# Attention stage: the scaled addition of the fetched expert results moves from VectorE to GpSimd, and the statistics after it one step later

## The reference, cut to what matters

```python
x = x + L0_attn(layernorm(x))
x = x + (y + shared)         # y: sum over a token's two experts of weight * expert result
x = x + L1_attn(layernorm(x))
x = x + L1_ffn(layernorm(x))
```

## Time and profile before

| what | value |
|---|---|
| median of 3 runs | 1394.51 us (1394.25 to 1395.08) |
| profiled execution | 1400.14 us |
| its span, first to last instruction | 1398.1 us |
| mean granted TensorE clock | 0.988 of full speed |
| busy: PE / DVE / ACT / POOL | 1336.1 / 688.0 / 489.1 / 448.3 us |

### The profile page before, as it was taken

How to read it: one execution, slowest core, us unless ns; L and a number is a source line. 1 busy time by engine, 2 the same in 40 slices (tenths; PEclk the granted TensorE clock), 3 DMA queues, 4 the chain that set the end, 5 groups by cost and what they waited for, 6 DMA issues and landing times.

```text
span 1398.1 us, 25005 instructions
## 1 busy us (share of the span) xinstructions
PE 1336.1 (96%) x8348; PEld 1036.2 (74%) x8348; DVE 688.0 (49%) x2499; ACT 489.1 (35%) x1046; POOL 448.3 (32%) x541
## 2 busy tenths in 40 slices
PE   7899999999999999999999999999998999999998
PEld 5566556688998998656666666666666788999998
DVE  5655457233333333337878888888887231310000
ACT  2221211122222222113666666666755412111111
POOL 2100000253222221242454454544323524343332
PEclk9999999999999999998999999999999999999999
DMA  9402011067777777243554554645442779999996
GB/s 327 129 31 72 4 41 43 22 220 234 234 243 238 237 236 226 67 120 100 143 155 140 148 154 130 181 116 150 146 128 75 273 289 312 346 333 344 332 347 210
DMA packets 95676, 254.29 MB, mean 182 GB/s; under 512 B 12189, under 2 KB 42271, under 8 KB 85568
## 3 DMA queue, kind: packets, MB, share of 16 engines
q1 hardware_dynamic: 79728, 217.61, 47.8%
q0 software_dynamic: 12096, 32.13, 7.4%
q10 hardware_dynamic: 3728, 2.97, 0.7%
HBM read 201.42 MB, written 52.17 MB: 181 GB/s over the span
## 4 chain that ended last, share of the span: by engine, by line
PE 84%; DVE 8%; issue 4%; ACT 2%; DMA 0%; DVEq 0%; ACTq 0%; POOLq 0%
PE psum L994 10%; PE psum L1004 10%; PE psum L675 10%; PE psum L813 10%; PE psum L796 7%; PE psum L686 6%; PE psum L851 4%; PE psum L898 4%; PE psum L873 4%; PE psum L922 3%; DVE work L1892 3%; PE psum L823 2%; PE psum L956 2%; PE psum L768 2%; PE psum L933 2%
## 5 line engine op out<-in xcount | busy, mean ns | idle before, releaser
L1892 DVE CUSTOM_DVE_ANT_0 work<-psum,mask 128x384 bf16<-128x384 f32 (+1 forms) x512 | 230.6, 485 | 59.3 <-PE psum L851 57.6
L851 PE MATMUL psum<-kz,qT 96*128 96x384 f32 (+1 forms) x512 | 167.3, 398 | 10.6 <-DVE small L1892 9.5
L1971 POOL DMA_INDIRECT work<-normed,token_of x71 | 67.5, 951 | 325.1 <-PE psum L768 198.2
L813 PEld LDWEIGHTS psum<-work,arena 128*128 128x128 f32 x1136 | 136.1, 193 | 15.7 <-ACT work L1148 11.0
L675 PE MATMUL psum<-arena 128*128 128x512 f32 x320 | 147.7, 600 | 0.0
L813 PE MATMUL psum<-work,arena 128*128 128x128 f32 x1136 | 143.6, 280 | 4.0 <-ACT work L1148 2.2
L994 PEld LDWEIGHTS psum<-arena 128*128 128x128 f32 x1248 | 145.5, 192 | 2.4 <-issue 0.4
L994 PE MATMUL psum<-arena 128*128 128x128 f32 x1248 | 146.2, 275 | 0.0
L1244 ACT ACTIVATE arena<-psum 128x384 f32<-128x384 f32 x256 | 112.2, 494 | 93.7 <-PE psum L873 92.8
L1004 PE MATMUL psum<-arena 128*128 128x256 f32 x624 | 143.1, 383 | 0.5 <-issue 0.5
L1746 DVE TENSOR_TENSOR arena<-psum,arena 128x256 f32<-128x256 f32 x39 | 16.6, 425 | 245.8 <-PE psum L1004 245.8
(11 more groups left out here) (243 smaller groups left out, 1993.0 us busy)
## 6 DMA issues: line engine op xcount, KB each, us to landing
arena<-in_w SPq DMA_DIRECT2D x78, 1024.0 KB
arena<-in_wgu SPq DMA_DIRECT2D x71, 704.0 KB, 5.0
strips<-hi SPq DMA_DIRECT2D x64, 256.0 KB
kz<-strips SPq DMA_DIRECT2D x64, 192.0 KB, 3.1
qT<-strips SPq DMA_DIRECT2D x32, 384.0 KB, 4.6
results<-work SPq DMA_DIRECT2D x71, 128.0 KB
strips<-lo SPq DMA_DIRECT2D x32, 256.0 KB
normed<-work SPq DMA_DIRECT2D x14, 512.0 KB, 3.1
```

Of the source, the lines that this page charges most:

```text
L813: m = e.matmul(psum[:, b % 2, q * P:(q + 1) * P], wu0[:, b % 4, c, q * P:(q + 1) * P], xsT0[:, b % 2, c * P:(c + 1) * P], start=(c == 0), ...
L851: m = e.matmul(psum[:, bk, at:at + w], qT[0:ROWS_S, slot, half, i * P:(i + 1) * P], kz[slot][0:ROWS_S, hd, lo_key:hi_key], start=True, sto ...
L1892: e.tensor_tensor_reduce(masked[:, n % 2, 0:w], psum[:, bank_of["scores", u, i, hd], at:at + w], mask[:, P - off:P - off + w], 1.0, MASKED ...
L1971: e.indirect_dma_start(out=xs[:, b % 3, :], out_offset=None, in_=normed[l][0:n, :], in_offset=bass.IndirectOffsetOnAxis(ap=token_of[:, l, ...
```

## The change

The addition goes from DVE to POOL. DVE's one instruction for each fetched tile becomes two on POOL: the fetched tile is multiplied by the weights in place, and, after a wait for that, added to X. They stand in POOL's step behind the masks and the fetch and ahead of the pads and of `pool_scale`; the steps are the same as before (-23 to -16). DVE keeps the statistics, one step later than before (after the second addition of a tile: steps -21, -19, -17 and -15 in place of -22, -20, -18 and -16), behind a wait for POOL's addition. Everything else, the fetches and the steps of all others among it, stays.

```diff
--- before.py
+++ after.py
@@ -397,10 +397,10 @@
             sem(n) for n in (
                 "picked", "counted", "so_far_made", "placed", "pick_step", "scored", "experts_listed", "list_set", "one_hot_made",
                 "rows_hot", "ones_made", "tokens_found", "tokens_listed"))
-        (pads_zeroed, key_pads_made, pads_made, moe_added, bias_added, v_made, hi_made, lo_made, maxima_placed,
+        (pads_zeroed, key_pads_made, pads_made, moe_added, got_scaled, bias_added, v_made, hi_made, lo_made, maxima_placed,
          mx_made, maxima_made, p_exped, p_masked, less_made, shift_made, oT_made, rec_made, o_made, oT2_act, oT2_dve, proj_added) = (
             sem(n) for n in (
-                "pads_zeroed", "key_pads_made", "pads_made", "moe_added", "bias_added", "v_made", "hi_made", "lo_made",
+                "pads_zeroed", "key_pads_made", "pads_made", "moe_added", "got_scaled", "bias_added", "v_made", "hi_made", "lo_made",
                 "maxima_placed", "mx_made", "maxima_made", "p_exped", "p_masked", "less_made", "shift_made", "oT_made", "rec_made",
                 "o_made", "oT2_act", "oT2_dve", "proj_added"))
 
@@ -1823,10 +1823,9 @@
                 if last:
                     for _ in links:
                         pass
-                for b, i in batch(s, -PRE - 7, 2 * TPB):
-                    t, j = b * TPB + i // 2, i % 2
-                    dve_add_fetched(e, t, j)
-                    if j == 1:
+                for b, i in batch(s, -PRE - 6, 2 * TPB):
+                    if i % 2 == 1:
+                        t = b * TPB + i // 2
                         e.wait_ge(moe_added, 2 * t + 2)
                         dve_stats(e, t)
                 for b, i in residual_due(s - 1):
@@ -1848,16 +1847,6 @@
                 return first_got[:, 2 * t + j, :], gathered[2 * t + j], 16
             k = 2 * (t - TPB) + j
             return c_got[:, k % 4, :], gathered[k % 4], 16 * (k // 4 + 2)
-
-        def dve_add_fetched(e, t, j):
-            src, got, n = got_slot(t, j)
-            if j == 0:
-                e.wait_ge(s_added, t // TPB + 1)
-            else:
-                e.wait_ge(moe_added, 2 * t + 1)
-            e.wait_ge(got, n)
-            e.scalar_tensor_tensor(X[:, t, 0:E], src, top_w[:, j, t:t + 1], X[:, t, 0:E], ALU.mult,
-                                   ALU.add).then_inc(moe_added, 1)
 
         def dve_v(e, b, t):
             if t == 0:
@@ -1997,6 +1986,17 @@
             e.indirect_dma_start(out=dst, out_offset=None, in_=results,
                                  in_offset=bass.IndirectOffsetOnAxis(ap=slot_of[:, j, t:t + 1], axis=0)
                                  ).then_inc(got, 16)
+
+        def pool_add_fetched(e, t, j):
+            src, got, n = got_slot(t, j)
+            if j == 0:
+                e.wait_ge(s_added, t // TPB + 1)
+            else:
+                e.wait_ge(moe_added, 2 * t + 1)
+            e.wait_ge(got, n)
+            e.tensor_scalar(src, src, top_w[:, j, t:t + 1], None, ALU.mult).then_inc(got_scaled, 1)
+            e.wait_ge(got_scaled, 2 * t + j + 1)
+            e.tensor_tensor(X[:, t, 0:E], X[:, t, 0:E], src, ALU.add).then_inc(moe_added, 1)
 
         def pool_key_pads(e, i):
 
@@ -2042,6 +2042,8 @@
                     m.then_inc(p_masked, 1)
                 for b, i in batch(s, -PRE - 10, 2 * TPB):
                     pool_fetch(e, b * TPB + i // 2, i % 2)
+                for b, i in batch(s, -PRE - 7, 2 * TPB):
+                    pool_add_fetched(e, b * TPB + i // 2, i % 2)
                 if s == -13:
                     pool_value_pads(e)
                     e.wait_ge(pads_made, 1)
```

## The result

The changed kernel takes 1426.55 us (median of four; 1424.67 the lowest) against 1394.38 us for the kernel before on the same chip: a ratio of 1.0221, 95% interval 1.0204 to 1.0238, 2.2% or some 31 us slower. One of the four took 1454.12 us at a lower granted clock (0.932 in place of 0.982 to 0.984) and isn't in the ratio. Forecast was +5.4 us. The side was right, the size was not, and the time lies outside the range. The profiled execution took 1426.87 us, 26.7 us over the profiled one of before.

What follows compares the result with a forecast made beforehand. PE was taken to bound the kernel, busy 96% of the span. Batch 0's wait 5.24, clock 1.7 and units -1.5 gave +5.4 us on 1394.51, so 1399.9 us; own range 1397 to 1403, whole range 1393.5 to 1406.0.

Steps and rivals of the forecast that it cites:

- What bounds the kernel: Whole kernel: PE is busy 96% of the span; batch 0's additions lie 0.24 us from the path that sets the end.
- Batch 0: Ahead of the units: POOL's last addition ends 5.48 us later, so PE stands still at L577 for 5.24 us.
- 585.30 + 8A: Time at which POOL's last addition of batch 0 ends, forecast at 595.62 us, against 590.14 on DVE.
- A: Cost of one addition on POOL, multiplication, wait and addition: 0.73 + 0.14 + 0.42 = 1.29 us, ends 0.64 and 3.16.
- the affine selects' line: POOL's one-input affine selects, 295 ns for 128 columns and 657 for 512, used to price the multiplication at 0.42 us.
- Nothing gives it back: Behind batch 0's wait PE's rows are gapless until 639.96 us, so the whole +5.24 us stays.
- The clock: PE's new idle in batch 0 lowers the granted clock: between 0 and +3.4 us, half taken, +1.7 us.
- The statistics only move by a step.: In the units, DVE's later statistics cost nothing; 0.43 us is added ahead of the scale, with PE's turn four steps later.
- the last rival: Statistics wait in the additions' place on DVE's path: -1.5 becomes +0.5, sum +7.4, 1401.9 us; chance within the forecast's 0.57.
- The masks on POOL: In the units, mask L2037 ends at 893.15 us, ahead of PE's need at 893.83: hidden, with 0.68 us left.
- The relief, -2.0 us: In the units, additions removed from DVE save five chain pieces of 0.40 us each.
- The port, +0.5 us: At the ends of 12 more units POOL's new work can hold up DVE, up to 0.73 us each; +0.5 taken.

Runs made afterwards that it cites:

- e1: Against the kernel before, only batch 0's additions move to GpSimd, its statistics one step later; batches 1 to 7 stay on VectorE: 1410.07 us, 1.0086.
- e6: The change with GpSimd's multiplication as a two-input operation, the weight broadcast over the columns: 1411.36 us, 1.0098 against the kernel before.
- e3: The change, but for batches 2 to 7 the statistics of all four tiles stand together in step -15: 1411.37 us, 1.0087 against the kernel before.
- e4: The kernel before, but VectorE adds only 8 of 256 columns of the fetched results in batches 2 to 7: 1396.68 us, 0.9994.
- e9: The kernel before with only GpSimd's bias addition moved to the end of its step, behind the masks and the scale: 1407.38 us, 1.0084.
- e10: The kernel before with GpSimd's bias addition split into four instructions, one for each tile, in the same place: 1391.54 us, 0.9977.
- e8: The change, but batches 0 and 1 added on VectorE and the other batches' statistics together in step -15: 1401.59 us, 1.0027 against the kernel before.

## Why the prediction was wrong, point by point

- *What bounds the kernel.* Right: batch 0's additions do lie a fraction of a microsecond from PE's path, and the relief on DVE lies off it. PE's rows behind L577 aren't gapless, as was said: it waits 0.73 us ahead of the second L922, in both kernels alike, so nothing hung on it.
- *Batch 0.* The mechanism, the place (L577) and the formula 585.30 + 8A were right; A was mis-sized. With the measured distance of 1.75 us from one multiplication's start to its addition's end (580.38 to 582.13) it gives 599.3 us, and 599.40 was measured; that it is so near is in part luck, as POOL's first addition began 0.25 us earlier than forecast and the fetches between the additions took some 0.08 us longer each. The wait is 9.40 us in place of 5.24. The fault is one term: the multiplication priced by the affine selects' line, 0.42 us, where 0.94 was measured. The sentence that both lines run between neighbouring sizes of the same engine hid that one of them is another operation.
- *Nothing gives it back.* Right: in e1 the 12 us are there to the end.
- *The clock.* Right in kind for batch 0, forecast +1.7; from the rows 2.6 us in e1 and, by +10.8 less 9.2 of shift, 1.6 in the change. That the size came so near was luck: 1.7 was half of an upper bound, and the wait was 1.8 times the forecast's. The lower clock behind the waits in the units was not in the sum.
- *In the units: "The statistics only move by a step."* This is the step that failed, and with it the last rival's "they should find it done". It is the larger part, 18.4 us, and the forecast's sum had nothing for it; the last rival named this wait, but let it cost no more than the relief it undoes, 2.0 us. I asked what is queued behind the new wait for batch 0, and for the units only whether POOL's masks come in time. The row that would have told is POOL's own queue: in five steps of a batch it has a fetch (0.95 us), on average one and a half masks of 0.64 us, and now an addition; with A = 1.75 and the gaps that is 3.9 us (3.87 in the mean of four steps, 856.90 to 872.36 us), against a mean step of 3.5. POOL falls behind, and the statistics, which stand in DVE's stream ahead of the next step's masks, turn that lag into idle time of DVE and then of PE. The mis-sized A made the lag larger, but is not likely its source: at e6's shorter addition (A = 1.43) DVE still waits 14.9 us, and a straight line from 29.6 through this gives some 8.5 at the forecast's 1.29, an estimate that no run tests.
- *The masks on POOL.* Right: with the lag of the change they still come before the last quarter of the values (872.99 against 875.50 in the stretch shown), and e3 loses no more than e1.
- *The relief, -2.0 us.* No gain was seen (e4; -2.4 to +0.8 us). That the five pieces of 0.40 us on the chain are no gain in waiting, because PE is then held by what stands second, fits this and is not shown.
- *The port, +0.5 us.* The collisions came, and PE paid next to nothing for them at the unit's end: in the change DVE's two maxima instructions take 15.7 and 8.6 us in all (13.9 and 5.8 before), while PE's waits for them are 8.5 us in place of 8.4. The masks, DVE's largest work, take no longer (229.9 against 230.6 us).

The Trainium skill (SBUF — State Buffer, "Who interferes with whom") says that a VectorE instruction with two SBUF inputs contends with GpSimd where GpSimd reads SBUF. The rows of e9 and e10 agree: L1646 and L1906 are such instructions and take 2.21 and 0.59 us beside the bias in place of 0.21 and 0.18.

## What to carry to other kernels

A wait that is added on an engine which walks through its code in order costs what is queued behind it, in each stage by itself: write out both queues, of the engine that now works and of the one that now waits, for the steady state as well as for the first turn. Where the consumer doesn't need the result yet, move its question back, not only by one step but until the producer's lag is covered; e3 got some 18 us back so. What is moved back together can hold up what stands behind it, as e8's rows show. And a price for an operation that the trace doesn't have belongs to the operation, not only to the engine: with a factor of two open on a term that counts eight times, the range has to hold it.

## What the runs showed of the hardware

On POOL a one-input multiplication of 128x256 f32 takes 0.94 us with a factor from a tensor and 0.87 with a fixed one; a two-input one with the factor broadcast takes 0.62, less than the addition's 0.73. Three VectorE instructions of some 0.2 us (L1646, L1904, L1906) take as long as the GpSimd addition beside them still runs, 2.2 us at the worst; a window mask that starts beside the same bias addition (924.17 us in the kernel before) takes its usual 0.42. Cutting GpSimd's one instruction of 2.36 us into four of 0.73 gave 0.23% of the whole time (0.12 to 0.34), though the four are together 0.47 us longer.
